# Router, residual and softplus of an audio tower's scan loop cut into small steps and dealt out over the half units

## The reference

```python
h = tokens(x)                        # conv of width 7, then a projection of 16 steps: 64 x 128 tokens of 256
h = h + mamba(layernorm(h))          # x @ W_in, causal conv of 4 taps, silu, x_ssm = xc @ W_xproj
#   delta = softplus(x_ssm[..., :1] * w_dt + b_dt);  A = -exp(A_log)
#   h_t = exp(delta * A) * h_(t-1) + delta * B * xc;  y_t = sum_n h_t * C;  (y + xc * D) * silu(z) @ W_out
logits = einsum('btc,ce->bte', x, w_gate)      # x = layernorm(h), 8 experts
gates = softmax(logits)
topk_vals, topk_idx = top_k(gates, 2)
combine = einsum('btk,btke->bte', topk_vals, one_hot(topk_idx, 8))
out = sum_e combine[:, e] * (silu(x @ wg[e]) * (x @ wi[e])) @ wo[e]
h = h + out
```

## Time and profile before

| | us |
|---|---|
| median of 3 runs | 3043.79 (3042.73 to 3047.66) |
| profiled execution | 3046.24 |
| its span, first to last instruction | 3044.5 |
| mean granted TensorE clock, share of full | 0.956 |
| first scan, last scan | 107.9, 2180.6 |
| one steady group, from scan 0 to scan 0 | 131.0 and 131.7 in turn |

### The profile page before, as it was taken

The page is one execution under the profiler, slowest core; times in us unless marked ns, Lnnn a source line. Parts: engine busy times, 40 slices in busy tenths (PEclk is TensorE's granted clock), DMA queues, the critical chain, the costliest instruction groups (busy, mean ns, idle before and its releaser), DMA issues. The chain is left out here.

```text
span 3044.5 us, 32684 instructions
## 1 busy us (share of the span) xinstructions
PE 2628.8 (86%) x7774; PEld 1299.6 (43%) x7775; DVE 2162.7 (71%) x2367; ACT 1469.8 (48%) x2717; POOL 1729.4 (57%) x864
## 2 busy tenths in 40 slices
PE   4689898888979889897888978887569999999999
PEld 2234343343434334343333434333236666666665
DVE  0599999989999998998999999999632222222222
ACT  2565656656555665665666565665212222222222
POOL 1566767777685767768676676777422222222222
PEclk9899899999999999999999999999879999999999
DMA  1321303223040321303123140321432222222222
GB/s 38 126 101 37 144 27 134 78 75 131 21 145 27 132 92 60 140 16 141 56 103 117 36 144 26 132 86 64 165 80 44 43 45 44 44 44 44 45 44 31
DMA packets 125600, 235.91 MB, mean 77 GB/s; under 512 B 46449, under 2 KB 93714, under 8 KB 109122
## 3 DMA queue, kind: packets, MB, share of 16 engines
q1 hardware_dynamic: 98342, 200.56, 19.2%
q0 software_dynamic: 26128, 34.36, 6.5%
q10 hardware_dynamic: 1036, 0.09, 0.0%
HBM read 182.22 MB, written 53.78 MB: 78 GB/s over the span
## 5 line engine op out<-in xcount | busy, mean ns | idle before, releaser
L536 POOL TENSOR_TENSOR arena<-u,arena 128x2048 f32<-128x2048 f32 x256 | 1157.9, 4528 | 357.2 <-DVE psum L927 355.9
L1244 PE MATMUL psum<-hc,ident 128*128 128x512 f32 x2048 | 1060.8, 645 | 272.6 <-DVE hc L935 272.4
L927 DVE TENSOR_TENSOR_SCAN psum<-psum,arena 128x1024 f32<-128x1024 f32 x512 | 1172.9, 2291 | 124.4 <-ACT psum L732 83.2
L1244 PEld LDWEIGHTS psum<-hc,ident 128*128 128x128 f32 x2048 | 379.7, 200 | 836.6 <-DVE hc L935 485.5
L732 ACT ACTIVATE psum<-delta,a_neg 128x508 f32<-128x508 f32 x1024 | 656.4, 674 | 0.6
L935 DVE TENSOR_TENSOR hc<-psum,arena 128x1024 f32<-128x1024 f32 x512 | 626.0, 1223 | 19.9 <-DVE psum L927 4.8
L615 POOL DMA_INDIRECT out_dram<-hres,tok_id x136 | 211.1, 1552 | 599.4 <-ACT hres L864 550.0
L1375 PE MATMUL psum<-arena,xnt 128*128 x1088 | 516.0, 597 | 0.0
L1129 DVE COPY z<-psum 128x512 f32<-128x512 f32 x136 | 94.1, 692 | 458.0 <-PE psum L1384 458.0
L864 ACT ACTIVATE hres<-psum,tok_w 128x256 f32<-128x256 f32 x136 | 64.3, 473 | 454.4 <-PE psum L1394 447.7
L1394 PE MATMUL psum<-arena,z 128*128 x1088 | 257.1, 379 | 0.9 <-DVE z L1129 0.9
(11 more groups left out here) (145 smaller groups left out, 1921.4 us busy)
## 6 DMA issues: line engine op xcount, KB each, us to landing
arena<-ssm_rows SPq DMA_DIRECT2D x128, 1024.0 KB, 5.9
delta<-expert_rows SPq DMA_DIRECT2D x136, 129.0 KB, 2.0
h_saved_rows<-hnew SPq DMA_DIRECT2D x16, 512.0 KB, 6.5
hres<-h_saved_rows SPq DMA_DIRECT2D x16, 512.0 KB
out_dram<-h SPq DMA_DIRECT2D x16, 512.0 KB, 3.0
draw<-ssm_rows SPq DMA_DIRECT2D x16, 256.0 KB, 3.2
arena<-in_L_ffn_wg_dram SPq DMA_DIRECT2D x8, 512.0 KB
arena<-in_L_ffn_wi_dram SPq DMA_DIRECT2D x8, 512.0 KB
```

Source lines behind the costliest of these rows:

```text
L536: pool.tensor_tensor(dBx[k % 2], rep, b_rep[:, q * QN:(q + 1) * QN, :], ALU.mult).then_inc(dbx_ready, 1)
L927: nc.vector.tensor_tensor_scan(h, h, src, 0.0, ALU.mult, ALU.add).then_inc(scan_done, 1)
L1244: last = nc.tensor.matmul(yacc[(k // HC) % 2], ident[:, :], hc[k % 2][:, i, :], start=False, stop=(k % HC == HC - 1 and i == 1))
```

## The change

- DVE: `residual` 0 behind product 5 and `residual` 1 between scan and product of half unit 8. `stats` is split: `aggregate` (bn_aggr) of the second norm goes inside half unit 10, that of the first inside 30, with its `bn_stats` behind 29.
- DVE: the router becomes 19 functions of one instruction (one has two). They stand inside (between scan and product) and behind half units 17 to 25. The first choice is taken from the logits (`ex >= 0`), the second from logits with the first lowered by 1e30; gates are `1 / sum` and `exp(second) / sum`, so that a second exponential (`second_gate`, ACT, 21) and a product in POOL's `second_row` come in. Scratch tiles move from PSUM to SBUF.
- PE: `count` at 23. POOL: `rsqrt` behind product 6, `first_row` behind 14, `scatter` behind 14 and 15. ACT: `router_exp` at 18; `softplus_abs` singly at 23 to 26, `_exp` at 27, `_ln` at 28, `_relu` at 26, 29, 30 and 31.

```diff
-        m1 = sb("m1", [P, 2, GB])
+        second = sb("second", [P, GB])
+        esecond = sb("esecond", [P, GB])
-        oh = [sb(f"oh{i}", [P, GB, E]) for i in range(2)]
+        oh = sb("oh", [P, 2, GB, E])
+        r_ex, r_key, r_rest, r_eq, r_pos = (sb(name, [P, GB, E])[:, :, :]
+                                            for name in ("r_ex", "r_key", "r_rest", "r_eq", "r_pos"))
+        r_at = sb("r_at", [P, 2, GB, E])[:, :, :, :]
+        r_slot = sb("r_slot", [P, 2, GB])[:, :, :]
-        r_ex, r_gates, r_key, r_g2, r_oh, r_pos, r_eq = (scratch(i) for i in range(7))
...
@@ gpsimd @@
-                pool.tensor_copy(row[:, :, C + 1:C + 2], m1[:, 1, :].rearrange("p (b a) -> p b a", a=1))\
-                    .then_inc(second_set, 1)
+                pool.wait_ge(second_exp, g + 1)
+                apart(pool, "pool")
+                pool.tensor_tensor(row[:, :, C + 1:C + 2], einv[:, :].rearrange("p (b a) -> p b a", a=1),
+                                   esecond[:, :].rearrange("p (b a) -> p b a", a=1), ALU.mult).then_inc(second_set, 1)
...
-                        if k == 5:
+                        if k == 6:
                             rsqrt(g - 1, 1, stat2, pow2)
-                        if k == 12:
+                        if k == 14:
                             first_row(g - 1)
-                        if k in (13, 14):
-                            scatter(g - 1, 0, 2 * (k - 13))
+                        if k in (14, 15):
+                            scatter(g - 1, 0, 2 * (k - 14))
@@ scalar @@
+            def second_gate(g):
+                actq.wait_ge(dv, ROUTER * g + 7)
+                ahead(actq, second_set, g)
+                nc.scalar.activation(esecond[:, :], second[:, :], ACT.Exp).then_inc(second_exp, 1)
...
-                    if k == 31 and not last:
-                        softplus_relu(g + 1, 3)
                     if k + 1 < HU:
                         exps(g, k + 1)
                     elif not last:
+                        softplus_relu(g + 1, 3)
                         exps(g + 1, 0)
...
-                        if k in (24, 25):
-                            softplus_abs(g + 1, k - 24)
-                        if k == 26:
+                        if k in (23, 24, 25, 26):
+                            softplus_abs(g + 1, k - 23)
+                        if k == 27:
                             softplus_exp(g + 1)
-                        if k == 27:
+                        if k == 28:
                             softplus_ln(g + 1)
-                            softplus_relu(g + 1, 0)
-                        if k == 28:
-                            softplus_relu(g + 1, 1)
-                            softplus_relu(g + 1, 2)
+                        if k in (26, 29, 30):
+                            softplus_relu(g + 1, (26, 29, 30).index(k))
@@ vector @@
+            def first_keys(g):
+                dve.wait_ge(lsub_ready, g + 1)
+                nc.vector.scalar_tensor_tensor(out=r_key, in0=ex[:, :, :], scalar=0.0, in1=key_w[:, :, :],
+                                               op0=ALU.is_ge, op1=ALU.mult).then_inc(dv, 1)
+            def largest_key(g, n):
+                after(g, n)
+                nc.vector.tensor_reduce(kmax[:, :], r_key, AX_X, ALU.max).then_inc(dv, 1)
+            def one_hot(g, n, k):
+                after(g, n)
+                nc.vector.tensor_tensor(oh[:, k, :, :], r_key, bc(kmax[:, :]), ALU.is_equal).then_inc(dv, 1)
+            def without_first(g):
+                after(g, 4)
+                nc.vector.scalar_tensor_tensor(out=r_rest, in0=oh[:, 0, :, :], scalar=-1.0e30, in1=ex[:, :, :],
+                                               op0=ALU.mult, op1=ALU.add).then_inc(dv, 1)
...
+            def second_equal(g):
+                after(g, 7)
+                nc.vector.tensor_tensor(r_eq, r_rest, bc(second[:, :]), ALU.is_equal).then_inc(dv, 1)
+            def second_keys(g):
+                after(g, 9)
+                nc.vector.tensor_tensor(r_key, r_eq, key_w[:, :, :], ALU.mult).then_inc(dv, 1)
+            def both_masks(g):
+                after(g, 12)
+                nc.vector.tensor_tensor(mask[:, :, :], oh[:, 0, :, :], oh[:, 1, :, :], ALU.add).then_inc(mask_ready, 1)
...
+            def chosen_positions(g):
+                after(g, 14)
                 for k in range(2):
+                    last = nc.vector.tensor_tensor(r_at[:, k, :, :], r_pos, oh[:, k, :, :], ALU.mult)
+                last.then_inc(dv, 1)
...
+            def slots_out(g):
+                after(g, 16)
                 nc.vector.tensor_copy(slot[:, :, :], r_slot).then_inc(slot_ready, 1)
...
                     if k in (11, 19, 27):
                         gate_y(g, (k - 11) // HC)
+                    if not first:
+                        if k == 8:
+                            residual(g - 1, 1)
+                        if k == 10:
+                            aggregate(g - 1, 1, stat2)
+                        if k == 17:
+                            router_max(g - 1)
+                        if k == 18:
+                            first_keys(g - 1)
+                        if k == 19:
+                            one_hot(g - 1, 3, 0)
+                        if k == 20:
+                            second_max(g - 1)
+                            exp_inverse(g - 1)
+                        if k == 21:
+                            second_keys(g - 1)
+                        if k == 22:
+                            one_hot(g - 1, 11, 1)
+                        if k == 24:
+                            positions(g - 1)
+                        if k == 25:
+                            slots(g - 1)
+                    if k == 30 and more:
+                        aggregate(g + 2, 0, stat1)
                     times_c(g, k)
                     if not first:
-                        if k == 6:
+                        if k == 5:
                             residual(g - 1, 0)
                         if k == 9:
-                            residual(g - 1, 1)
                             stats2(g - 1)
                         if k == 17:
-                            router_a(g - 1)
-                        if k in (19, 20):
-                            for part in ((0, 1), (2,))[k - 19]:
-                                router_b(g - 1, part)
+                            router_sub(g - 1)
+                        if k == 18:
+                            largest_key(g - 1, 2)
+                        if k == 19:
+                            without_first(g - 1)
+                            exp_sum(g - 1)
+                        if k == 20:
+                            second_equal(g - 1)
+                        if k == 21:
+                            largest_key(g - 1, 10)
                         if k == 22:
-                            router_c(g - 1)
-                    if k == 28 and more:
+                            both_masks(g - 1)
+                        if k == 24:
+                            new_counts(g - 1)
+                            chosen_positions(g - 1)
+                        if k == 25:
+                            slots_out(g - 1)
+                    if k == 29 and more:
                         stats1(g + 2)
@@ tensor @@
-                        if k == 21:
+                        if k == 23:
                             count(g - 1)
```

More of the change, by code:

```diff
@@ L774, in front @@
                     evac_h(1, m)
-                softplus_abs(0, 0)
-                softplus_abs(0, 1)
+                for c in range(NCH):
+                    softplus_abs(0, c)
                 softplus_exp(0)
@@ L903, in stats, with aggregate @@
                 ins.then_inc(stat_step[which], 1)
+            def aggregate(g, which, ready):
                 dve.wait_ge(stat_step[which], g + 1)
@@ L1028, in front @@
                 stats1(0)
+                aggregate(0, 0, stat1)
                 dve.wait_ge(s_aexp, 1)
@@ L1064, in tail @@
                 stats2(g)
-                router_a(g)
-                for part in range(3):
-                    router_b(g, part)
-                router_c(g)
+                aggregate(g, 1, stat2)
+                router_max(g)
+                router_sub(g)
+                first_keys(g)
+                largest_key(g, 2)
+                one_hot(g, 3, 0)
+                without_first(g)
+                exp_sum(g)
+                second_max(g)
+                exp_inverse(g)
+                second_equal(g)
+                second_keys(g)
+                largest_key(g, 10)
+                one_hot(g, 11, 1)
+                both_masks(g)
+                positions(g)
+                new_counts(g)
+                chosen_positions(g)
+                slots(g)
+                slots_out(g)
             front()
```

92 lines of the change are left out of this document (36 added, 56 removed).

## The result

The changed kernel takes 3059.02 us, median of 6 runs (3056.77 to 3059.90); the kernel before, 6 runs beside it, 3045.18 us. The ratio is 1.0045, 95% interval 1.0032 to 1.0057: slower by 13.8 us. The profiled execution took 3059.86 us with a span of 3058.0.

The account below looks back on a forecast made before the run. The prediction took VectorE (DVE), 93% busy in the 130.8 us steady groups, as the bound. Its parts summed to +1.5 us a group, +19.5 for 13 groups, +27.5 with the others: 3071 us, given as 3070, range 3005 to 3108.

Parts of the forecast that it names:

- the four places: DVE waits for POOL's product: first_keys at 18, one_hot at 19 (4.1 us) and 22 (1.0), slots_out at 25 (3.4).
- part 1: Scans 5 to 11: earlier residual and aggregate inside a half unit shorten waits, -3.0 us a group.
- part 2: Scans 17 to 26: dealt-out router steps with SBUF tiles wait for POOL, +2.1 us to scan 21, +2.8 after.
- part 4: POOL's queue: later scatters delay the next group's products, scan 4 waits, +0.6 us a group; scan 0 in time.
- the small step: Price of a small DVE step: 0.20 us behind a product, 0.03 us taken between scan and product.
- ACT's chain holds scan 21: Scan 21 waits for ACT whatever DVE does, so removing the old steps of 19 and 20 wins little.
- the lock: SBUF-only DVE steps share an exclusive port with POOL; one coming second waits for the rest of POOL's 4.53 us product.
- Part 3: Scans 26 to 0: softplus in single pieces, statistics behind 29, aggregate inside 30, -1.0 us a group.
- Outside: Groups outside the steady sum: group 14 +3 extra, group 15 +6, group 0 -1 us.
- Rival B: Only two-input SBUF steps wait, the cast at 25 does not: 3027 us, faster; chance 0.18.
- C: DVE is not held by a running POOL product, or gets in between its pieces: 2981 us; chance 0.12.
- D: POOL falls behind, its first product 5 us later in 14 groups, +35 us more: 3106 us; chance 0.10.

Follow-up runs that it names:

- e2: The changed kernel with only r_slot, the input of the cast, in PSUM: 3029.76 us, ratio 0.9953.
- e10: The changed kernel with the second choice's scatters moved behind POOL's products 3 and 5 of the next group: 3043.54 us, ratio 1.0003.
- e9: e1 with the second choice's scatters moved behind POOL's products 3 and 5 of the next group: 2964.66 us, ratio 0.9741.
- e1: The changed kernel with the router's scratch, all but r_ex, back in PSUM, order of steps unchanged: 2998.49 us, ratio 0.9845.
- e4: The changed kernel with one_hot ahead of the gate at half unit 19, tiles still in SBUF: 3041.47 us, ratio 0.9995.
- e12: e9 with the first one_hot written to PSUM too and the positions written twice: 2962.23 us, ratio 0.9733.
- e3: The changed kernel with only r_key, one input of both one_hot steps, in PSUM: 3026.86 us, ratio 0.9944.
- e6: The kernel before with only the softplus in single pieces, first-norm statistics behind 29 and their aggregate inside 30: 3028.04 us, ratio 0.9949.
- part 1 alone: The kernel before with only the residuals behind 5 and inside 8, aggregate inside 10, POOL's square root one product later: 3001.44 us, ratio 0.9860.
- e11: e4 with the second one_hot moved behind product 22 and slots_out behind product 26, all tiles in SBUF: 3001.16 us, ratio 0.9868.

## Why the prediction was right, and where its terms were off

The sign, the mechanism and the four places were as forecast; the size was +13.8 us instead of +27.5, as part 1 gave less than forecast and part 2 cost less. The sign hung on little: without the cast's wait the kernel is faster than before (e2, ratio 0.9953), and without POOL's late head it is the same (e10, 1.0003). By the steps of the prediction, in us a group:

- **Part 1**: forecast -3.0, measured -2.27. The step is right: without a late POOL it is -2.8 (24.67 in e9 and e10). What is missing is that part 4 reaches into it: in the groups where scan 4 waits 2 us, the residual behind product 5 then waits 0.34 to 2.03 us for PE, 0.46 in the mean of the 13. The wait for scan 10, about 1.1 us by the forecast's own terms, is 1.10.
- **Part 2**, 17 to 21: forecast +2.1, measured +1.23. Half unit 17 is 4.23 us instead of 3.69, since max now comes before PE's router products are done and waits 0.60. That moves first_keys closer to the end of POOL's product, so 18 is 3.87 instead of 4.7. The largest term holds: one_hot takes 4.14 us, 4.1 was forecast, and 19 is 8.18 for 8.5. Half unit 20 is 3.57 for 3.8.
- **Part 2**, 21 to 26: forecast +2.8, measured +2.27. The second one_hot 1.18, slots_out 3.45 us, forecast as waits of 1.0 and 3.4. The mis-sized term is the small step: from the last step behind a product to the next scan it is 0.09 us (830.39 to 830.48), and two steps cost 0.19 (838.47 to 838.66, worked out from the same timeline), not 0.20 each. My price came from a pair in the earlier trace rows of which the second reads the result of the first. PSUM has no part in it: e1 has the same.
- **ACT's chain holds scan 21**: argued ahead of the run, and doubted by me after e1 and e4, where the stretch stood at 18.72 without any wait for ACT. e12 shows it true: 2.67 us of waits for ACT come back. That e1, e3 and e4 had come out at the forecast 18.6 was luck: there it was the lock on without_first that ended just behind ACT.
- **Part 3**: forecast -1.0, measured -1.05 from 26 to 0: 0.86 in half units 28 to 30 and 0.18 in 26. But the forecast had left out what the later softplus does to POOL: in e6 the stretch 0 to 5 takes 0.65 us more.
- **Part 4**: forecast +0.6 from scan 4 alone, measured +0.78 from 0 to 5, and some 0.5 more in the stretch 5 to 11 (25.21 against 24.67), 15.5 us in all (e10). Scan 0 was in time, as forecast (the terms of its t(25) + 22.8 add up to 22.6, which changes nothing). The cause was named too narrowly. In the changed kernel add_delta does start directly behind the scatters, but e6 grows by 0.65 us in the same stretch with the scatters where they were. No run has the new places of first_row and the scatters alone, so how the 0.78 divides between them and part 3 is open; e10 shows only that moving the second scatters away removes it.
- **Outside**: 13 groups by 0.96 us are 12.5. Group 15 was forecast at +6 and is +2.6 (120.87 to 123.43); Group 14, forecast at 1.5 + 3, grew by 3.63 (126.48 to 130.11) and is one of the 13. Between them and the span's difference, 13.5 us, lie -1.6 us in groups 0 and 1 and behind the last scan.

Rival B falls by e2, C by the four rows above. D was half right: POOL does fall behind, but that is 15.5 us in all, not 35. Taken apart by the runs: part 1 alone -41.9 us, part 3 alone -15.3, together -57 if they add; the router and POOL's queue turn this into +13.8, so they cost 71. The lock, in the steps that PSUM frees, is worth 78.9 us (e10 to e9), the queue 15.5 (e10) to 34 (e9 against e1). As these two come to more than 71, dealing out the router is no loss in itself; what it alone gains wasn't run, and how far the gains of parts 1 and 3 add is open.

## What to carry to other kernels

Where POOL runs long products beside DVE, a small DVE step with all its inputs in SBUF can cost the whole rest of the product; keep one input in PSUM (the output does not help, e1), or put the step where POOL is idle or just ahead of its product (e1 and e11 give the same 3000 us). Look for it in mean durations that don't fit the tile, not among the waits. When a wait has gone and the stretch hardly shrinks, the next one may be another of its kind or a different engine: take both away before you name the bound, and look at a group in which one of them is missing.

## What the runs showed of the hardware

- A one-input cast of 128 x 8 fp32 to uint32, SBUF to SBUF, is held by POOL's product as a two-input step is: 3.25 us in the mean, 0.16 when its input is in PSUM (e2) or POOL is idle (e11). The Trainium skill, "SBUF — State Buffer", section "Who interferes with whom", says that a copy or cast in a two-port mode takes the shared port; these rows agree, and for so small a cast as well, though no row shows in which mode it ran.
- Whoever comes first goes through. In e4 one_hot starts 0.16 us ahead of POOL's product (828.18, 828.34) and takes 0.17; in the changed kernel it comes 0.43 behind (833.27, 832.84) and takes 4.14. In the changed kernel second_keys starts at 844.43, 0.16 ahead of the product at 844.59, and takes 0.17 too. POOL loses nothing by one_hot in e4: its product starts 2.36 us after scan 19 in both (825.98, 830.48).
- A short idle time of PE can cost more behind it, and does not always. In e1, scan 4 of group 7 waits 2.75 us for POOL. Timeline of PE behind it, and table by stretches around it (columns as in the earlier trace rows, clock third from the end):

```profile
1015.82 3.03 PE L1328 MATMUL psum<-hc,ident 128*128 128x512 f32 x4 [2.60 <-DVE hc L946]
1018.64 2.58 PE L1340 MATMUL psum<-w_out_sb,yz 128*128 128x256 f32 x8
1021.50 1.88 PE L1328 MATMUL psum<-hc,ident 128*128 128x512 f32 x4
1023.22 1.89 PE L1340 MATMUL psum<-w_out_sb,yz 128*128 128x256 f32 x8
```

```profile
1008.00:1012.00 4.00, 4.00 (x13) 1.90 (x12) 1.42 (x2) 2.22 (x5) 4.00 (x1) 1.00 0.17 42
1012.20:1015.80 3.60, 1.02 (x5) 0.56 (x3) 3.56 (x3) 1.42 (x5) 3.13 (x3) 1.00 0.27 80
1015.80:1021.30 5.50, 5.48 (x15) 3.37 (x16) 3.43 (x3) 1.39 (x3) 5.50 (x2) 0.69 0.08 9
1021.30:1030.00 8.70, 8.70 (x35) 5.68 (x34) 8.63 (x6) 3.76 (x8) 7.14 (x4) 1.00 0.04 4
```

The granted clock is 1.00 up to the idle 2.6 us, 0.69 in the mean of the 5.5 us behind them, so for a part of them at the lower of its two levels, 1.2 GHz, and 1.00 again. The same matmuls take 1.15 and 0.69 us longer than in the two rows below them: a wait of 2.6 us is one of 4.4, the residual waits 2.03 us for PE, and the stretch 5 to 11 takes 26.80 us. But in group 13 of e1 PE idles just as long, the clock stays at 1.00, the residual waits 0.34 us and the stretch takes 25.11:

```profile
1782.77 1.99 PE L1328 MATMUL psum<-hc,ident 128*128 128x512 f32 x4 [2.57 <-DVE hc L946]
```

In all 13 groups of both kernels the residual's wait goes with the clock: 2.03 us or more where the mean from scan 4 to scan 6 is 0.82 or 0.83, at most 0.51 where it is 1.00. What decides whether the clock falls is not the length of the idle time alone (2.02 us with a fall in group 5 of the changed kernel, 2.08 without in group 7), and no run here shows it.

The prediction feared this fall at half unit 19, where PE idles 4 us, and it is there. Timeline of PE in the changed kernel, group 5, and the stretch behind the idle time:

```profile
838.60 2.85 PE L1325 MATMUL psum<-hc,ident 128*128 128x512 f32 x4 [3.82 <-DVE hc L943]
```

```profile
838.70:842.20 3.50, 3.50 (x5) 0.88 (x6) 3.50 (x6) 2.64 (x4) 0.00 (x0) 0.62 0.00 0
```

The clock of half unit 20 is 0.62 in the mean of the 13 groups, 1.00 before; in half unit 24 it is 1.00, 0.53 before. The mean of the stage, 0.95 for 0.96, hides that the fall has moved. It costs nothing at its new place, as no scan from 20 to 26 waits in the changed kernel.
